# Four-layer graph network on one core: the last layer's edges sorted into destination buckets on chip, gathered rows summed by one-hot products, all eight relations weighed ahead

## The reference

```
x = LN(x + gcn(x))                       # layer 0
x = LN(x + sage2(x))                     # layer 1: two times  h @ W_self + mean_of_neighbours(h) @ W_neigh + b
x = LN(x + attention(x))                 # layer 2: rms norm, W_down (1024 to 256), 4 heads, segment softmax, @ W_up
def last(x):                             # layer 3
    u = x @ root + bias
    for r in range(8):
        mask = (edge_type == r)
        sums = segment_sum(x[src] * mask[:, None], dst)
        cnt  = segment_sum(mask, dst)
        u = u + (sums / maximum(cnt, 1)[:, None]) @ weight[r]
    z = concatenate([u, x]) @ w_gate + b_gate
    return tanh(u) * z + x * (1 - z)
x = LN(x + last(x))
```

## Time and profile before

| | us |
|---|---|
| median of 3 executions | 3857.01 |
| lowest, highest | 3836.16, 3875.2 |
| span of the profiled execution | 3698.9 |
| busy in it: PE, DVE, POOL, ACT | 3462.3, 2038.9, 1363.0, 939.7 |
| between span and median | 158.1 |

### The profile page before, as it was taken

One profiled execution on the slowest core, in us unless ns is written; L12 is line 12 of the kernel. 1 busy time (PEld: TensorE's weight loads), 2 busy tenths in 40 slices (PEclk: granted clock), 3 DMA queues, 4 the chain that ended last, 5 costly groups with the idle time before them and its releaser, 6 DMA issues.

```text
span 3698.9 us, 55829 instructions
## 1 busy us (share of the span) xinstructions
PE 3462.3 (94%) x22823; PEld 2642.5 (71%) x22823; DVE 2038.9 (55%) x4393; ACT 939.7 (25%) x1365; POOL 1363.0 (37%) x1094
## 2 busy tenths in 40 slices
PE   5898868999999999989989979899999999999998
PEld 4566556899899899934434478677777777777798
DVE  7877656432433454364443367777676544444477
ACT  0112313111211312222222266342222122222134
POOL 3767625566455567757777211300000000000021
PEclk8999989999999999989999989999999999999999
DMA  8789785543643455544554355543432422222233
GB/s 286 197 258 280 252 288 145 158 123 82 180 120 95 138 179 163 165 146 158 167 165 137 113 220 186 175 178 108 147 128 74 143 78 82 71 82 72 70 109 107
DMA packets 268704, 557.27 MB, mean 151 GB/s; under 512 B 94954, under 2 KB 118143, under 8 KB 266430
## 3 DMA queue, kind: packets, MB, share of 16 engines
q1 hardware_dynamic: 124504, 384.00, 29.6%
q10 hardware_dynamic: 64520, 116.89, 8.9%
q0 software_dynamic: 79424, 52.83, 8.8%
HBM read 370.13 MB, written 183.44 MB: 150 GB/s over the span
## 4 chain that ended last, share of the span: by engine, by line
PE 70%; DVE 11%; DMA 7%; POOL 6%; issue 4%; ACT 2%; SPq 1%; ACTq 0%; POOLq 0%; DVEq 0%
PE ps L442 50%; PE ps L825 11%; DMA EM<-ee,adr 2%; POOL EM L2483 2%; PE ps L447 2%; POOL gl L2493 2%; POOL gr L2493 2%; DVE eqj L989 2%; DVE eqj L986 2%; DMA slab<-T 1%; PE ps L710 1%; PE ps L712 1%; PE ps L711 1%; PE ps L491 1%; PE ps L492 1%
## 5 line engine op out<-in xcount | busy, mean ns | idle before, releaser
L442 PE MATMUL ps<-a,yy 128*128 128x384 f16 (+5 forms) x3200 | 429.2, 296 | 10.4 <-DVE yy L1685 9.0
L442 PE MATMUL ps<-wb,xh 128*128 128x256 f16 (+1 forms) x2560 | 427.7, 274 | 8.3 <-DVE xl L1257 5.4
L825 PE MATMUL ps<-mh,whl 128*128 128x384 f16 (+5 forms) x2048 | 426.3, 301 | 8.3 <-DVE ml L1832 7.5
L2444 POOL DMA_INDIRECT TR<-cnt,adr x167 | 277.2, 1660 | 362.0 <-DMA TR<-cnt,adr 345.7
L2533 POOL TENSOR_TENSOR graw<-graw,rsb 128x1280 f32<-128x1280 f32 (+1 forms) x2 | 5.7, 2854 | 1098.7 <-DMA graw<-GD 1098.7
L442 PEld LDWEIGHTS ps<-a,yy 128*128 128x128 f16 (+1 forms) x3200 | 311.6, 98 | 127.2 <-DVE yy L1685 9.3
L442 PE MATMUL ps<-wb,xl 128*128 128x256 f16 (+1 forms) x1280 | 350.2, 274 | 0.0
L710 PE MATMUL ps<-sl,x 128*128 128x512 f16 (+1 forms) x800 | 308.0, 385 | 29.8 <-ACT ue L2165 23.0
L2444 POOL DMA_INDIRECT T<-cnt,adr x167 | 271.9, 1628 | 133.6 <-DMA T<-cnt,adr 78.3
L711 PE MATMUL ps<-sl,x 128*128 128x512 f16 (+1 forms) x800 | 307.6, 384 | 0.0
L712 PE MATMUL ps<-sl,x 128*128 128x512 f16 (+1 forms) x800 | 307.4, 384 | 0.0
(11 more groups left out here) (355 smaller groups left out, 6913.1 us busy)
## 6 DMA issues: line engine op xcount, KB each, us to landing
TR<-zero_w SPq DMA_DIRECT2D x80, 625.0 KB, 4.7
EM<-neg ACTq DMA_DIRECT2D x40, 625.0 KB, 3.5
wraw<-in_L_gnn_weight SPq DMA_DIRECT2D x48, 512.0 KB, 3.3
UD<-ue ACTq DMA_DIRECT2D x90, 256.0 KB, 3.1
uu<-UD SPq DMA_DIRECT2D x45, 512.0 KB, 6.2
ar<-TR SPq DMA_DIRECT2D x72, 320.0 KB
eb<-EM SPq DMA_DIRECT2D x9, 2500.0 KB, 10.1
ar<-TR SPq DMA_DIRECT2D x72, 305.0 KB
```

The source lines that it names most:

```text
L442: i = pe.matmul(ap, l, r, start=(q == 0), stop=(q == len(pairs) - 1))
L825: ins = pe.matmul(ps[:, 0:cn], l, r, start=(q == 0), stop=(q == len(pairs) - 1))
L2444: return pool.indirect_dma_start(out=flat, out_offset=bass.IndirectOffsetOnAxis(ap=adr[:, n, t:t + 1], axis=0), in_=cnt[:, n, t:t + 1], in ...
```

## The change

All eight relations are weighed ahead (`NBR = NFR = 8`): `fold` takes 128 steps, there are 16 `u` groups with a ring of 16 slabs, and eight builds. The table `TR`, its fill, adds and reads, the second `equal_keys`, the 16 steps of root and gate weights on x2, and all dense products of the last layer go, as do the transposed sums.

In their place the edges are sorted by destination tile. While the first layer runs, DVE makes one-hots of each edge's (destination, relation) cell and PE multiplies them (`counts`); the reciprocals go to the table `CT`, 128x80. In the second SAGE layer's first quarters DVE computes every edge's place in ten buckets padded to 512 (`edge_places`). POOL gathers each edge's share from `CT` and scatters a record of 16 bytes (row in `YD`, column in its tile, share) into `PT`. After the attention's heads POOL makes 204 one-hots (edge by destination within its tile) and stores them in `OH`. The builds write all weighed rows to `YD` (8x1250 rows of 4 KB). Then `GROUPS = 51` groups of `GT = 4` tiles of 128 edges follow: POOL gathers the rows (places without an edge hold an index out of bounds and are skipped), ACT and DVE split them, PE sums them by one-hot products, DVE adds a group's PSUM into `sums` at an offset that it loads from `turns`. Root and gate weights on x3 (`late_unit`, 40 units of 24 matmuls) run between the builds and beside the groups. The gate at the end has ten steps of 48 matmuls. In steps, the diff cut to its core:

```diff
-NBR = 5
-
-NFR = 5
+NBR = 8
+
+NFR = 8
...
-NS, NU = 11, 4
+NS, NU = 16, 4
...
+GROUPS, GT = 51, 4
+TILES = GROUPS * GT
+NPAD = TILES * 128
+NGB, NUB, NYB, NOH, NZX, NLW = 6, 5, 3, 4, 3, 4
+for n in range(AHEAD, 30):
+    BESIDE[44 * (n - AHEAD) // 27].append((1 + n // NT, n % NT))
...
+            def cell_hot(c):
...
+                for to, v, width in ((cell_a, key, 128), (cell_b, cnt, 80)):
+                    dve.tensor_tensor(to[:, 0:n, :], v[:, 1, t0:t0 + n, None].broadcast_to([EP, n, width]),
+                                      wide[:, None, 0:width].broadcast_to([EP, n, width]), ALU.is_equal).then_inc(
...
+            def late_unit(u, i):
...
+                for k in range(8):
+                    t = ls[LATE_SET[u]][k]
+                    w.wait_ge(*V("late", 8 * u + k))
+                    pe.matmul(ps[0:r, :], x3t[:, k, 0, c], t[:, 0, :], start=(k == 0), stop=False)
+                    pe.matmul(ps[0:r, :], x3t[:, k, 0, c], t[:, 1, :], start=False, stop=False)
+                    ins = pe.matmul(ps[0:r, :], x3t[:, k, 1, c], t[:, 0, :], start=False, stop=(k == 7))
...
+            for g in range(GROUPS):
+                for j in range(2):
+                    psum.take("sums", g, j)
+                w.wait_ge(*oh_in[g % NOH](g))
+                for m in range(GT):
+                    t = GT * g + m
+                    w.wait_ge(*V("yl", t))
+                    for h in range(2):
+                        for j in range(2):
...
+                            ins = pe.matmul(psum.at("sums", g, j)[:, :], hot[g % NOH][:, m, :],
+                                            yp[t % NGB][:, h, 512 * j:512 * j + 512], start=(m == 0 and h == 0),
+                                            stop=(m == GT - 1 and h == 1))
+                    ins.then_inc(*P.tick("used", t))
...
+            def add_u(r, i):
+                n, rk = NT * r + i, ROWS[i]
+                w.wait_ge(*u_in[n % NUB](n))
...
+            def low_gathered(t):
+                a = t % NGB
+                w.wait_ge(*A("yh", t))
+                dve.scalar_tensor_tensor(out=yp[a][:, 1, :], in0=yg[a][:, :], scalar=recs[:, t, 2:3], in1=yp[a][:, 0, :],
+                                         op0=ALU.mult, op1=ALU.subtract).then_inc(*V.tick("yl", t))
+
+            def add_sums(g):
+                first = dve.value_load(turns[0:1, g:g + 1], min_val=0, max_val=D * (NT - 1))
+                w.wait_ge(*P("sums", g))
+                w.wait_ge(*V.now())
+                for j in range(2):
+                    to = sums[j][:, bass.ds(first, 512)]
+                    dve.scalar_tensor_tensor(out=to, in0=psum.at("sums", g, j)[:, :], scalar=yscale[:, 0:1], in1=to,
+                                             op0=ALU.mult, op1=ALU.add).then_inc(*psum.taken_out(V, "sums", g, j))
...
+                act.mul(yp[a][:, 0, :], yg[a][:, :], recs[:, t, 2:3]).then_inc(*A.tick("yh", t))
...
+            w.wait_ge(*P("y3", NREL - 1, 9, 1))
+            for t in range(TILES):
+                a = t % NGB
+                if t >= NGB:
+                    w.wait_ge(*V("yl", t - NGB))
+                pool.indirect_dma_start(
+                    out=yg[a][:, :], out_offset=None, in_=YD, in_offset=bass.IndirectOffsetOnAxis(ap=recs_i[:, t, 0:1], axis=0),
+                    bounds_check=NREL * N - 1, oob_is_err=False).then_inc(*rows_y[a].tick(t))
```

More of the change, by code:

```diff
@@ L34 @@
 BASE = 16512
[L35 removed]
+NX, NL, NZ, NB, NPT, LAG = 4, 4, 10, 3, 11, 5
 NG, LAST_B = 3, (ET - 1) // NB
@@ L470, in degrees, with counts @@
                 i.then_inc(*P.tick("degs", c))
+            def counts(c):
+                if c == 0:
+                    psum.take("ct", b=3)
+                    w.wait_ge(*psum.empty("ct"))
+                w.wait_ge(*V("cells", c))
+                for m, t in enumerate(COUNTED[c]):
+                    i = pe.matmul(psum.at("ct")[:, 0:80], cell_a[:, m, :], cell_b[:, m, :], start=(t == 0), stop=(t == ET - 1))
+                i.then_inc(*P.tick("ct", c))
             def project(n):
@@ L631, in tensor @@
                                   stop=True).then_inc(*P.tick("bsc"))
+                    if layer == 0 and q == 1:
+                        ps = psum.take("place")
+                        w.wait_ge(*V("rtot"))
+                        w.wait_ge(*psum.empty("place"))
+                        pe.matmul(ps[:, 0:NT], above[:, :], rtot[:, :], start=True, stop=True)
+                        pe.matmul(ps[:, 16:16 + NT], onesf[:, 0:1].broadcast_to([128, 128]), rtot[:, :], start=True,
+                                  stop=True).then_inc(*P.tick("place"))
                     if layer == 0 and q == 2:
@@ L811, in weigh @@
[L811 to L826 removed]
+            ps = psum.take("smx")
@@ new lines, in turn_x3 @@
+            def turn_x3(i):
+                w.wait_ge(*A("x3", i))
+                turn_rows("x3T", i, z3[i])
+            build(0)
+            ps = psum.take("sc")
+            w.wait_ge(*V("scale"))
+            w.wait_ge(*psum.empty("sc"))
+            pe.matmul(ps[:, 0:2], smx[0:2, NREL:].broadcast_to([2, 128]), ident[0:2, 0:2], start=True,
+                      stop=True).then_inc(*P.tick("sc"))
+            build(1)
+            for i in range(5):
+                turn_x3(i)
+            build(2)
@@ L926, in rsqrt @@
+            turn_u(0)
+            for i in range(NT):
+                if i + 1 < NT:
+                    turn_u(i + 1)
+                gate(i)
         def rsqrt(dve, w, y, v, t, *key):
@@ new lines, in scalar, with high_u, tanh_u @@
+            for s in zx_out:
+                s.at["last",] = s.n
+            def high_u(i):
+                r = ROWS[i]
+                for h in range(2):
+                    w.wait_ge(*P("uT", i, h))
+                    if i >= 2:
+                        w.wait_ge(*P("zg", i - 2, 1))
+                    copy(uT[i % 2][:, 0, 4 * h:4 * h + 4, 0:r], four(psum.at("uT", i, h), r), "uT", i, h)
+            def tanh_u(i):
+                r = ROWS[i]
+                w.wait_ge(*V("u"))
+                if i >= 2:
+                    w.wait_ge(*V("mixed", i - 2))
+                act.activation(th[i % 2][0:r, :], sums[0][0:r, D * i:D * i + D], ACT.Tanh).then_inc(*A.tick("tanh", i))
```

1645 lines of the change are left out of this document (716 added, 929 removed).

## The result

| | median us | runs |
|---|---|---|
| before | 3851.24 | 4, 3836.16 to 3875.2 |
| changed | 3991.01 | 4, 3961.07 to 4013.78 |

The changed kernel is slower: ratio 1.0377, 95% interval 1.0316 to 1.0438. The forecast was 3470, with a range of 3345 to 3690. Its profiled execution took 3998.33 us, and its span is 3996.6: only 1.7 us lie outside the span.

A forecast was written before the change was run, and what follows sets the result against it. PE was taken to bound the kernel before, DVE the new groups; 2334 + 15 + 18 + 360 + 10 + 425 + 150 = 3312 us of span, with 158.1 outside it 3470; range 3345 to 3690.

The forecast's parts named there:

- The step that failed: Shares, times and records beside the SAGE layers: 667 us of POOL DMAs, PE waits for none, price nothing.
- The second failed step: Whole kernel: 158.1 us outside the profiled span, kept and added to the forecast span of 3312.
- Up to the first tables: Start until the first layer's tables: more folds, second comparison gone, counts added; +15 us (0 to +40).
- the `u` stage: From 1305 to 2138: six more `u` groups replace root and gate; +18 us (+5 to +45), some 850 us.
- The last layer: From 2334 to the end: 1365 us become 945.
- builds: Eight builds in the last layer: PE 313 us, DMA 297; 360 us (330 to 420), DMA share 0.9 or more.
- turning: Barrier between the last build and the gathered tiles: last store, gather landing and split; 10 us (5 to 20).
- groups: The 51 groups in the last layer: DVE longest at 409 us, 16 for waits; 425 us (380 to 530).
- gate: End of the last layer: ten tiles of 13.2 us, start and norm's tail; 150 us (140 to 165).
- offset load: DVE's load for each of 51 PSUM adds: 0.74 us taken, between 0.17 and 3.1; 38 us in all.
- Gathers: Rival, last layer: landing of gathered rows bounds the 51 groups; 541 us, 3586 in all, or 612, 3657; chance 0.12.
- the queue: Rival, last layer: POOL's queue serves one 512 KB gather after another, 6.2 us each; 1265 us, 4310 in all; chance 0.04.

The follow-up runs named there:

- the three series' alone: Changed kernel with four small POOL memsets ahead of each DMA of the shares, times and records, no wait for landings: 3420.85 us.
- the one profiled again: The kernel before, unchanged, run again with a profile: 3830.08 us, span 3828.3.
- timed paused version: Changed kernel with four POOL memsets ahead of each share, time and record DMA, two ahead of each attention row gather: 3351.54 us, ratio 0.8706.

## Why the prediction was wrong

**The step that failed** is the sentence on POOL's series, "3 x 167 DMAs at 1.03 + 0.30 ... Nothing on PE waits for them ... Price: nothing while this holds". The period was about right (1.25 to 1.30 measured against 1.33), and that nothing on PE waits for them is right too. But the price was taken from who waits for whom, and not from what a DMA series without waits does to the others. 790 us were lost ahead of the last layer where 33 were forecast. The pauses take back 640 of the whole time (3991.01 to 3351.54), the three series' alone some 570 (3991.01 to 3420.85). By what the DMAs hold up the other engines stays open. Every one of these executions has a recorded span and clock, so whether an unrecorded one starves in the same way is not shown either. The earlier trace rows held a hint that I read the wrong way: POOL's wait of 345.7 us for `TR` adds to land was counted as waste that the change removes. The runs fit its having kept the traffic apart: the same gathers of times cost PE nothing to be seen between adds that wait (627 us busy of 644, from 604 to 1248), and 227 us in a row.

**The second failed step** is "outside the span lie 158.1 us, which I keep". Spans and times agree within 3.4 us in every later run. The first profile was a short execution, so the row totals and the median described two different things. In it the row gathers beside the `u` slabs did little harm; in the one profiled again the stage was 124 us longer. Why the first execution was spared, no run shows. The sum should have been made against the median by raising that stage, and the difference taken as a warning of something in the kernel that varies.

**Up to the first tables, and the `u` stage.** In the timed paused version PE first transposes `lt`, in the middle of the SAGE layers, at 976.4; before, at 933.5. The first products with the table's slabs already start 42 us later (494.2 against 452.1). So the first part costs 43 us more where +15 was forecast and +40 was the high end; which of its terms was too small is not shown. Another 46.3 us are PE's wait behind POOL's paused series. From the first row gather to the last `ue` (1402 to 2279) it took 877 us against 850 forecast, after the pauses.

**The last layer** was right in what bounds it, and its sum too high, 880 against 945: builds 340 (360 forecast; DMA share 0.83, not 0.9), turning 13 (10, the one term that was too low), groups 389 (425), gate 137.6 (150). DVE was the longest engine in the groups, as forecast, though PE was as busy (343.74 and 341.44 of 389). The offset load, taken at 0.74 us between 0.17 and 3.1, is short (queue rows: minimum/median/maximum ns):

```profile
L1733 DVEq TENSOR_LOAD <-turns x51: 300/304/548, 3480.8 to 3855.2; - x51
L1733 DVEq FUSED_REGOPS  x51: 190/190/216, 3481.4 to 3855.5; - x51
```

0.49 us together, 25 for the 51. DVE's idle time right ahead of the adds is only 10.5 us in all, so most of it lay under the instruction before. The floor of about 600 ns that the prediction cites from the Trainium skill, "DMA: Bandwidth & Descriptors", was nearer than my value, but the load here, at 304 ns, lies below it. The splits took 1279 ns (1282 taken) and the adds 746 (739).

**The rivals.** Gathers did not bound the groups (ACT waited 96.6 us for them in pieces, beside DVE's work); the clock in the groups was 0.97 at 88% busy; the queue did not serve one gather at a time (204 of them in 389 us are 1.9 us each, against the 6.2 of that rival). The forecast of slower rested on the last alone, so its 0.04 was for a cause that did not occur. What did occur was not among the rivals: the indirect DMAs were looked at where they are large and waited for, not where they are small, many and free.

**Luck.** With the pauses the time, 3351.54, is under 3470 and inside the stated range, but that was not the kernel asked about, and part of the nearness is chance. As a span the forecast was 3312, and the paused version's is 3347, by two errors against each other: `z3` ended at 2468, 108 later than forecast, and what follows took 879 us, 73 less. Only the 158 us added for outside the span put 3470 above it.

## What to carry to other kernels

A wait on POOL for an indirect DMA's landing may be what protects the other engines (seen here with 128 rows of 4 or 16 bytes a DMA, and to a lesser degree with rows of 1 KB); whoever removes it should look at the rate of DMAs that results, and space the DMAs (work on POOL, or interleaving with others) before adding waits, which cost POOL's time. When the span of the profiled execution and the median differ by much more than the 2 to 3.4 us seen here, the profile may be of another execution than the typical one, and the stage in which they differ is worth finding first. An engine that is idle for "issue", with the granted clock at its lower level and the DMA share near zero at once, was here held up by another engine's DMAs; its own waits do not name them.

## What the runs showed of the hardware

- Indirect DMAs of POOL with 128 rows of 4 or 16 bytes, one per 1.25 us without waits, brought PE to one instruction per 1.4 us and all DMA traffic together to 12 to 37 GB/s, while the DMA engines' recorded share was 0.06 to 0.13. At one per 1.43 to 1.50 the harm was partial, at 1.62 and above absent in these stretches.
- A limit on the number in flight was not what counted: a limit of four starved the rest (3951.48), none at all with pauses did not (3420.85).
- Gathers of 1 KB rows and scatters, three in about 5.0 us in the kernel before, did a smaller harm of the same look, 79 us (3799.75 without, 3720.98 with pauses). They differ in size and waits, so the edge for them is not known.
- Gathers of 4 KB rows in the groups, 204 in 384 us, did no such harm.
- Why PE's instructions are slowed is not settled. All engines and the loads suffer together, and no run took them apart. Nor was it tried whether fewer rows in a DMA, at the same rate, would do.
